# Graph layers kernel: batches of 15 and 12 tiles for 14 and 13, ten positions of the late block summed, first mix moved

## What is computed

```python
x1 = x_nodes[src].reshape(-1, N_SEG, EXTENT)          # 16 segments of 32
x2 = x_edges.reshape(-1, N_SEG, EXTENT)
i1, i2, i3 = (path_indices[:, 0], path_indices[:, 1], path_indices[:, 2])   # 64 paths
contrib = path_coeffs[None, :, None] * x1[:, i1, :] * x2[:, i2, :]
edge_out = zeros.at[:, i3, :].add(contrib)
out = zeros.at[dst].add(edge_out.reshape(-1, OP_SIZE))
...
h = maximum(_layernorm(x), 0)
x = x + second_layer(h, edge_attr_512, ...)
```

## Time and profile before

| | us |
|---|---|
| median of 3 runs | 1072.91 (1070.64 to 1081.23) |
| the profiled execution | 1072.47 |
| its span, first to last instruction | 1070.8 |
| VectorE busy | 897.5 (84%) |
| TensorE matmuls busy | 829.7 (77%) |
| GpSimd busy | 492.3 (46%) |
| ScalarE busy | 444.3 (41%) |

### The profile page before, as it was taken

How to read it: one execution, slowest core, us unless ns; L and a number is a source line. 1 busy time by engine, 2 the same in 40 slices (tenths; PEclk the granted TensorE clock), 3 DMA queues, 4 the chain that set the end, 5 groups by cost and what they waited for, 6 DMA issues and landing times.

```text
span 1070.8 us, 22798 instructions
## 1 busy us (share of the span) xinstructions
PE 829.7 (77%) x5046; PEld 394.0 (37%) x5053; DVE 897.5 (84%) x2196; ACT 444.3 (41%) x1685; POOL 492.3 (46%) x572
## 2 busy tenths in 40 slices
PE   1688887996167787868788987878797787887878
PEld 0343443442022443524243443424344243443426
DVE  4677668843069999999999999899998999999894
ACT  3888887432401523425161432416133261522423
POOL 4211220443634546566454657546564564646400
PEclk9999999998578898898889888888987889888788
DMA  9000000043555656687665657666565775767610
GB/s 166 1 0 0 0 0 2 15 192 124 165 229 204 229 177 238 233 284 249 240 239 187 235 195 275 255 219 245 188 233 195 254 256 182 247 188 241 225 21 10
DMA packets 59517, 183.03 MB, mean 171 GB/s; under 512 B 20116, under 2 KB 20244, under 8 KB 54972
## 3 DMA queue, kind: packets, MB, share of 16 engines
q0 software_dynamic: 27616, 87.97, 26.1%
q1 hardware_dynamic: 22568, 88.88, 22.3%
q10 hardware_dynamic: 9268, 5.55, 1.9%
HBM read 173.71 MB, written 8.66 MB: 170 GB/s over the span
## 4 chain that ended last, share of the span: by engine, by line
PE 26%; DVEq 21%; DVE 20%; issue 17%; ACT 6%; POOL 4%; DMA 2%; ACTq 1%; SPq 1%; another core or an unknown queue 1%; POOLq 0%
DVE q_mem L858 16%; PE psum L1226 15%; DVEq L850 10%; DVEq L853 5%; PE psum L1211 4%; DVEq L858 4%; PE psum L1129 3%; ACT S L1059 3%; PE psum L1140 2%; DVE x_mem L748 2%; ACT hot_mem L1046 2%; DMA x_mem<-in_L_gnn_W 1%; PE psum L1126 1%; POOL x_mem L622 1%; POOL spare L515 1%
## 5 line engine op out<-in xcount | busy, mean ns | idle before, releaser
L858 DVE TENSOR_TENSOR q_mem<-x_mem 128x448 f32 (+2 forms) x1392 | 725.6, 598 | 68.3 <-DMA x_mem<-h_rows,src_now 31.6
L1226 PE MATMUL psum<-q_mem,hot_mem 128*32 128x512 f32 x2584 | 424.4, 714 | 136.6 <-DVE q_mem L858 79.4
L622 POOL DMA_INDIRECT x_mem<-h_rows,src_now x323 | 390.8, 1210 | 174.3 <-issue 94.5
L1059 ACT ACTIVATE S<-psum,coef 128x32 f32<-128x32 f32 (+1 forms) x800 | 147.5, 335 | 301.4 <-issue 133.6
L1226 PEld LDWEIGHTS psum<-q_mem,hot_mem 128*32 128x32 f32 x2584 | 107.5, 126 | 414.5 <-issue 294.1
L1211 PEld LDWEIGHTS psum<-S,place 128*128 128x128 f32 x1600 | 187.8, 194 | 45.9 <-issue 45.7
L1211 PE MATMUL psum<-S,place 128*128 128x32 f32 x1600 | 195.2, 278 | 11.8 <-issue 11.5
L748 DVE TENSOR_SCALAR x_mem<-x_mem,spare 128x320 bf16<-128x320 f16 x323 | 77.8, 299 | 42.0 <-issue 42.0
L1071 ACT ACTIVATE acc<-psum 128x512 f32<-128x512 f32 x12 | 7.2, 597 | 201.4 <-PE psum L1211 201.4
L1140 PE MATMUL psum<-x_mem,hot_mem 128*128 128x320 bf16 x323 | 67.2, 321 | 28.8 <-DVE x_mem L748 20.3
L953 ACT ACTIVATE hot_mem<-x_mem,spare 128x128 bf16<-128x128 f16 x240 | 74.9, 388 | 20.5 <-PE psum L1140 20.0
(11 more groups left out here) (187 smaller groups left out, 437.8 us busy)
## 6 DMA issues: line engine op xcount, KB each, us to landing
x_mem<-in_edge_attr SPq DMA_DIRECT2D x60, 768.0 KB
x_mem<-in_edge_attr SPq DMA_DIRECT2D x35, 1024.0 KB
x_mem<-h_rows,src_now POOLq DMA_INDIRECT x323
out<-acc POOLq DMA_DIRECT2D x12, 256.0 KB, 4.3
x_mem<-in_x SPq DMA_DIRECT2D x1, 2304.0 KB
out<-x_mem ACTq DMA_DIRECT2D x9, 256.0 KB
h_rows<-x_mem ACTq DMA_DIRECT2D x9, 256.0 KB, 2.0
x_mem<-in_L_gnn_W SPq DMA_DIRECT2D x1, 1024.0 KB, 13.9
```

Source lines behind the costliest of these rows:

```text
L622: pool.indirect_dma_start(x1[:, j * TB + t, :], None, h2_dram[:, :], bass.IndirectOffsetOnAxis(ap=now, axis=0)).then_inc(landed, 16)
L858: return nc.vector.tensor_tensor(q[s % 2][:, 0:tiles, p % PG:p % PG + 1, :], x1_segs[:, first:first + tiles, ds(a, 1), :], x2_segs[:, firs ...
L1059: last = nc.scalar.activation(S[:, p * U:(p + 1) * U], sums, ACT.Copy, scale=coef[:, p:p + 1])
L1226: last = nc.tensor.matmul(ps[s % G][side * M:(side + 1) * M, :], hot[:, j * TB + k, :], q[s % 2][:, k, :, :].rearrange("p n u -> p (n u)") ...
```

## The change

The first three sides have four tiles in batch 0, so the batches have 15 and 12 tiles (15 and 11 in the last item). `sum_slot` sums block 3 in two parts: positions 0 to 9 always, and positions 10 to 15 only if more than 58 positions are kept. Block 0 is mixed behind slot 4 and not behind slot 5. VectorE reads the next item's number of turns behind slot 4 of the item before. TensorE reads `n_kept` into a register ahead of the turns, and waits for all 15 tiles' rows before its twelve warming matmuls.

```diff
--- before.py
+++ after.py
@@ -27,8 +27,8 @@
     S4 = 4
     M = P // S4
     NORMAL, LAST_ITEM = [7, 7, 7, 6], [7, 7, 6, 6]
-    CUT = [[(0, 4), (0, 4), (0, 3), (0, 3)], [(4, 7), (4, 7), (3, 7), (3, 6)]]
-    CUT_LAST = [[(0, 4), (0, 4), (0, 3), (0, 3)], [(4, 7), (4, 7), (3, 6), (3, 6)]]
+    CUT = [[(0, 4), (0, 4), (0, 4), (0, 3)], [(4, 7), (4, 7), (4, 7), (3, 6)]]
+    CUT_LAST = [[(0, 4), (0, 4), (0, 4), (0, 3)], [(4, 7), (4, 7), (4, 6), (3, 6)]]
     T = max(NORMAL)
     TI = sum(NORMAL)
     TB = sum(b - a for a, b in CUT[0])
@@ -53,11 +53,13 @@
     PG = NP // G
     LATE = 14
     SURE = NP - LATE
+
+    EDGE = 10
     assert SURE > (G - 1) * PG
     TURN = 2 * G
 
 
-    MIX_AT, MIX_LAST = {1: [G - 1], 0: [G - 2], G + 1: [0], 2 * G - 1: [1]}, {1: [G - 1], 0: [G - 2], G + 1: [0], G + 2: [1]}
+    MIX_AT, MIX_LAST = {1: [G - 1], 0: [G - 2], G: [0], 2 * G - 1: [1]}, {1: [G - 1], 0: [G - 2], G: [0], G + 2: [1]}
     MIX_END = [G - 2, G - 1]
     RING = 2 * T
     ROWS_A = 5
@@ -878,13 +880,16 @@
                         nc.vector.memset(pause[:, cell:cell + M // 2], 0.0)
                 last.then_inc(multiplied, 1)
 
-            def product_turn(again, turn):
+            def product_turn(again, turn, next_item):
                 for j in range(2):
                     n = tiles_before(CUT[j])[-1]
                     wait_rows(dve, x1_in[j], turn, n)
                     dve.wait_ge(x2_in[j], turn * (16 * S4) + 16 * S4)
                     for g in range(G):
                         product_slot(turn, j * G + g, g, j * TB, n)
+                        if j and g == 0:
+                            many_next = item_turn_count(next_item)
+                return many_next
 
             def product_last(again, turn):
                 for j in range(2):
@@ -894,9 +899,19 @@
                     for g in range(G):
                         product_slot(turn, j * G + g, g, j * TB, n)
 
-            for item in range(ITEMS - 1):
-                product_turns(dve, item, turn_count, product_turn)
-            product_turns(dve, ITEMS - 1, turn_count, product_last)
+            def item_turn_count(item):
+                return dve.value_load(meta[0:1, TURNS + item:TURNS + item + 1], min_val=1, max_val=WINDOWS * PLACES)
+
+            many = item_turn_count(0)
+            for item in range(ITEMS):
+                with dve.Fori(0, many) as again:
+                    turn = dve.snap(turn_count, min_val=0, max_val=ITEMS * WINDOWS * PLACES - 1)
+                    if item < ITEMS - 1:
+                        many_next = product_turn(again, turn, item + 1)
+                    else:
+                        product_last(again, turn)
+                    dve.reg_add(turn_count, turn_count, 1)
+                many = many_next
             total = dve.snap(**all_placed(turn_count))
             dve.wait_ge(rows_back, 16)
             dve.wait_ge(mixed, total + 1)
@@ -1194,10 +1209,10 @@
 
             pe.wait_ge(items_ready, 2)
             pe.wait_ge(paths_ready, 1)
+            kept_n = pe.value_load(n_kept, min_val=SURE, max_val=NP)
             segs = [pe.alloc_register(f"segs_{n}") for n in range(WORDS[1])]
             pe.load(segs, packed[0:1, WORDS[0]:WORDS[0] + WORDS[1]])
-            for i in range(2):
-                pe.wait_ge(x1_in[0][i], 16 * (TB // 2))
+            wait_rows(pe, x1_in[0], 0, TB)
             for n in range(12):
                 nc.tensor.matmul(ps[5][0:M, 0:COLS], iota_f[:, :], dst_rel, start=True, stop=True)
 
@@ -1219,14 +1234,23 @@
                 if s == 0:
 
                     pe.wait_ge(saved, turn * G + 2)
-                for t in range(max(b - a for a, b in cut)):
-                    for side, (a, b) in enumerate(cut):
-                        if t < b - a:
-                            k = at[side] + t
-                            last = nc.tensor.matmul(ps[s % G][side * M:(side + 1) * M, :], hot[:, j * TB + k, :],
-                                                    q[s % 2][:, k, :, :].rearrange("p n u -> p (n u)"),
-                                                    start=(j == 0 and t == 0), stop=(j == 1 and t == b - a - 1))
-                last.then_inc(summed, 1)
+
+                def add(first, end):
+                    for t in range(max(b - a for a, b in cut)):
+                        for side, (a, b) in enumerate(cut):
+                            if t < b - a:
+                                k = at[side] + t
+                                last = nc.tensor.matmul(ps[s % G][side * M:(side + 1) * M, first * U:end * U], hot[:, j * TB + k, :],
+                                                        q[s % 2][:, k, first:end, :].rearrange("p n u -> p (n u)"),
+                                                        start=(j == 0 and t == 0), stop=(j == 1 and t == b - a - 1))
+                    return last
+
+                if s % G < G - 1:
+                    add(0, PG).then_inc(summed, 1)
+                else:
+                    with pe.If(kept_n > NP - PG + EDGE):
+                        add(EDGE, PG)
+                    add(0, EDGE).then_inc(summed, 1)
 
             def sum_turn(turn, cuts, mix_at):
                 for j in range(2):
```

## The result

The kernel after took 1185.07 us (median of four runs, 1181.64 to 1194.79) against 1071.85 for the kernel before: ratio 1.105, 95% interval 1.0958 to 1.1142. The forecast was 1065.0 with a range of 1055 to 1082, 7.5 us faster. The measured change is 113 us slower: the other sign and fifteen times the size. The profiled execution has a span of 1193.1 us, 122.3 more than before.

A forecast was written before the change was run, and what follows sets the result against it. VectorE was taken as the bound, with only 36.8 us of idle time in the turns to be won. The terms +0.3 - 1.7 - 5.0 - 0.6 - 0.5 = -7.5 us took 1072.5 to 1065.0 us, range 1055 to 1082.

The forecast's parts named there:

- Products: VectorE's products: 58 products at 15 and 12 tiles take 60.3 us a turn, as at 14 and 13; nothing gained.
- The wait at slot 0: VectorE's wait for sum 6 at each turn's first product: 10.0 us idle in eleven waits, 8.9 saved.
- Block 0's mix behind sum 4: TensorE's mix ahead of sum 5 makes slot 7 wait: 0.6 us a turn, 7.2 lost, ends 0 and 20.
- Rival B: The mix on the way to sum 5 bounds batch 1: 2.2 us idle a turn at slot 7, 1084 us; chance 0.14.
- The batches: Gathers and loads with 15 and 12 tiles: +0.3 us at the start, -0.6 from small gaps before slot 4.
- Ten positions: Sums 3 and 7 stream 320 columns: 0 in the turns, 1.0 us at the very end; the branch costs 0.
- The early turn count: VectorE's early read of the next item's turn count lies in the queue's lead: 0, ends -2 and +4.
- Turns with long waits: Idle time at slots 2 to 4 of slow turns shrinks: 3.2 and 1.8, 5.0 us saved, ends 2 and 8.
- The end: After the last slot 6: sum 7 loses 1.0 us, but sum 6 starts 0.3 to 1.7 late; value -0.5.
- Rival C: Starved instruction streams from TensorE's longer loop: three more turns with stalls at 4.8 us, 1079 us; chance 0.13.
- A's case: Sum 5 is always in time, so no idle time at slot 7 and 7.2 us not lost: 1058 us; chance 0.15.
- D: Shorter sums don't show since the matmuls' issue, not the columns, bounds them; the rest cancels: 1073 us; chance 0.08.

The follow-up runs named there:

- e5: The kernel before, unchanged, run and profiled again in the session of the experiments: 1046.9 us, ratio 0.9993.
- e6: The kernel after, unchanged, run and profiled again in the session of the experiments: 1132.2 us, ratio 1.0819 to the kernel before.
- e8: The kernel before with batches of 15 and 12 tiles and idle matmuls (12 and 8) ahead of slots 4's and 5's waits: 1068.1 us, ratio 1.023.
- e7: The kernel after with idle TensorE matmuls, 12 ahead of slot 4's wait and 8 ahead of the save's: 1075.0 us, ratio 1.0269 to the kernel before.
- e13: The kernel before with block 0's mix behind sum 4 and 8 idle matmuls each ahead of slot 4's wait and the save's: 1075.3 us, ratio 1.027.
- e4: The kernel before with only the batches of 15 and 12 tiles and their wait: 1070.8 us, ratio 1.0215.
- e9: The kernel before with only the ten positions of sums 3 and 7 and their branch: 1060.0 us, ratio 1.0014.
- e3: The kernel after without the branch of sums 3 and 7 and the six positions in it: 1134.0 us, ratio 1.0818 to the kernel before.
- e18: The kernel before with three idle matmuls of 160 columns inside block 0's mix: 1134.1 us, ratio 1.0532.
- e1: The kernel after with block 0's mix back behind sum 5: 1080.2 us, ratio 1.0305 to the kernel before.

## Why the prediction was wrong

**What bounds the kernel** was right: VectorE, and only its idle time can be won. 26.9 + 9.8 us of it was all there was, and in e5 9.4.

**Products: right but for the spacing.** Forecast 0; the products take 5.4 us more between e5 and e6.

**The wait at slot 0: right in kind, half in size.** Forecast 10.0 to 1.1 us; it became 4.9 in both profiles of the kernel after. All eleven waits of e6 are 0.41 to 0.62 us and end 3.5 to 4.1 us behind sum 6. They are VectorE's own way round, a term that the prediction put at nothing; without the early turn count it is 1.06 or more (e8).

**Block 0's mix behind sum 4: this step failed.** The prediction put 14.0 to 14.8 us against 15.04 and took 0.6 us a turn, 7.2 in all, with 20 as the far end. e6 has 5.5 to 6.5 us a turn, 71.8 in all. By terms: sum 4 4.1 forecast, 4.6 measured; save 2.98, 3.1; zeroing and mix 4.1, 7.5; sum 5 2.8, 5.35; from there to VectorE 0.55, 1.06. The whole is 14.5 forecast and 21.6 measured. Mix and sum 5 carry 5.95 of the 7.1 us, and both are one error: the mix was priced at the clock that it had behind a sum. In the new order it stands behind a wait for ScalarE of 3.2 us. In e6 the clock fell in that wait, the mix ran at the lower level in every turn and sum 5 in eleven of the twelve; in e7, with the wait filled, the mix took 3.8 us in every turn. Another 0.5 us is the hand-over: the prediction took slot 0's 0.55 for it and counted the five jumps of the late slots as free, which they are not behind a wait. The earlier trace rows had shown the lower clock right behind a mix. The prediction gave it to part of sum 5 alone. The far end should have been mix and sum 5 both doubled: 14.8 + 3.8 + 2.8 = 21.4, an idle time of 6.9 a turn with the 0.55 and against the 15.04. That bound was to be had from the earlier trace rows.

**Rival B had the mechanism** (the mix on the way to sum 5 as the bound of batch 1), with 2.2 us a turn and a chance of 0.14; its size falls by the same term, since it doubled no mix. The Trainium skill, TensorE: Matmul & The Clock Gate, Part 1, was quoted beside it: the lower clock is the state at rest and activity lifts it. e7 agrees, 8.2% down to 2.7%. The same runs show its limit: in e13 the clock fell with TensorE busy.

**The batches** were priced only by loads and by the sums' lengths at either clock, never by what thinner sums do to the clock. e4 shows 2.2% for them, with sum 5 at 4.6 us in the mean and a floor of 1.06 us under each wait at slot 0. In the kernel after this is hidden in the mix's price: they can't be added up, since 1.076 and 1.022 would give 1.10 and not 1.082.

**Ten positions: right** (e9, 1.0014; sums 3 of 320 columns at 2.35 us as forecast), and the branch is free (e3). **The early turn count** was 0 with an upper end of 4: 5.4 us at slot 5 in e6, against which stands the shorter way at slot 0 (0.41 us for 1.06, eleven times). **Turns with long waits:** the waits vanished as forecast, but they were the session's, not the kernel's, and they were misread. The 2.02 us was put down to VectorE lacking work; it was released by the semaphore of sum 7, 7.2 us behind that sum's end, and all four turns with idle time at slot 2 follow such a semaphore. **The first product** came 0.07 us later in e6 than in e5, where 1.25 were forecast. **The end** was to be 0.5 shorter and was 0.8 longer in e6. **Rival C** (starved streams) fits what the first session adds, 30.4 us at slot 6 and the step from 1.082 to 1.105; that a stream starves isn't shown. A's case, no idle time at slot 7 at the higher clock, is seen in four turns of e13 and nowhere in the kernel after; D has no support.

Of 18 runs none beats the kernel before.

## What to carry to other kernels

Here a wait of 3 us put ahead of TensorE's work was paid twice, once as the wait and once in the lower clock of what stood behind it (mix 7.04 us for 3.76, sum 5 5.35 for 2.78). So price every matmul between the new wait and the one that is awaited at both levels, the unmoved ones too. Count what is serial between two hand-overs from the awaited end backwards: here sum, save, mix and sum took 14.7 us at the higher level (e13) and 20.5 with mix and last sum at the lower (e6), for 15 to 16 us of cover. Less work was not less time, as the sums of 12 tiles showed. And a wait may hide another right behind it: look at what the engine does between the awaited end and its next instruction, in a turn where the awaited one is early.

## What the runs showed of the hardware

- A sum of 24 matmul records took 5.35 us (e4) where one of 26 took 3.63: the shorter one ran at the lower clock. At the higher, 24 take 2.78 (e7).
- The granted clock fell from 1.00 to 0.50 in the middle of a mix, with TensorE busy in the whole window (e13, 724 to 730), in eight turns of twelve, and stayed at 1.00 in the other four with the same instructions. Windows of the kernel before, e5, show it behind the mix too:

```profile
714.00:717.00 3.00, 3.00 (x28) 3.00 (x28) 3.00 (x8) 2.64 (x15) 2.41 (x2) 1.00 0.61 178
717.00:720.00 3.00, 2.58 (x18) 1.13 (x21) 3.00 (x8) 0.00 (x0) 1.44 (x2) 0.74 0.66 173
```

- A semaphore of TensorE came up to 10.4 us after the last matmul's end in the first session and up to 13.4 in e18, in stretches where the DMA share was 0.84 to 1.02, and at most 0.1 us after it in e1 to e6. The same two kernels differ by 10.5% in the one and by 8.2% in the other. A single session's profile shows waits that another's doesn't have.
- Three idle matmuls a turn inside one mix went with 5.3%, by gaps of 0.48 us and more between matmuls of another mix, and with the late semaphores ahead of it (e18). The cause is open.
